# An adaLN block with latent attention and routed experts: the front part and the attention put into one block

## What is computed

```
mod = (silu(c) @ wmod).reshape(1, 6, 1, -1)
sa, ca, ga, sb, cb, gb = (mod[:, n] for n in range(6))
ga = (2 * (ga >= 0) - 1) * maximum(abs(ga), 0.25)            # gb alike
h = layernorm(x) * (1 + ca) + sa
q = rms_norm(h @ w_qa, q_a_norm_w) @ w_qb                    # 16 heads of 128 + 64
kv = h @ w_kva;  c_kv, k_rope = kv[..., :64], kv[..., 64:]
kv_up = rms_norm(c_kv, kv_a_norm_w) @ w_kvb                  # 16 heads of 128 (keys) + 128 (values)
q_rope, k_rope = apply_rope(q_rope), apply_rope(k_rope)
attn = softmax(causal(q_full @ k_full.T / sqrt(192)))
x = x + ga * ((attn @ v) @ w_o)
```

## Time and profile before

| | us |
|---|---|
| median of 3 runs | 1189.31 |
| lowest and highest | 1188.31 and 1192.61 |
| the profiled execution | 1187.94 |
| its span, first to last instruction | 1186.0 |

### The profile page before, as it was taken

One profiled execution on the slowest core, in us unless ns is written; L12 is line 12 of the kernel. 1 busy time (PEld: TensorE's weight loads), 2 busy tenths in 40 slices (PEclk: granted clock), 3 DMA queues, 4 the chain that ended last, 5 costly groups with the idle time before them and its releaser, 6 DMA issues. The chain is left out here.

```text
span 1186.0 us, 27727 instructions
## 1 busy us (share of the span) xinstructions
PE 1124.4 (95%) x11356; PEld 936.1 (79%) x11356; DVE 819.1 (69%) x1825; ACT 791.4 (67%) x1104; POOL 698.9 (59%) x579
## 2 busy tenths in 40 slices
PE   4869999999999999999999999999999878999997
PEld 4746878888888888888888888888887777989886
DVE  2758776767767777776767677776767466675776
ACT  3725777778777778778777787877877644233332
POOL 1434767678786867768777776877776762130000
PEclk8967999999999999999999999999999989999999
DMA  9250100002001000200100020011000060000000
GB/s 241 73 150 12 47 20 2 19 2 65 20 2 47 20 19 2 65 5 16 47 19 20 2 65 2 20 36 31 20 2 1 2 178 1 1 19 1 19 19 18
DMA packets 58350, 39.89 MB, mean 34 GB/s; under 512 B 8145, under 2 KB 57553, under 8 KB 58065
## 3 DMA queue, kind: packets, MB, share of 16 engines
q1 hardware_dynamic: 56832, 34.10, 10.1%
q10 hardware_dynamic: 1392, 4.03, 1.3%
HBM read 33.66 MB, written 4.46 MB: 32 GB/s over the span
## 5 line engine op out<-in xcount | busy, mean ns | idle before, releaser
L880 POOL TENSOR_TENSOR pt_lo<-pt 128x1024 f16<-128x1024 f32 x192 | 370.3, 1939 | 181.7 <-ACT pt L937 181.4
L993 DVE TENSOR_REDUCE gates<-bank 128x1 f32<-128x512 f32 x384 | 261.5, 688 | 147.7 <-PE bank L1060 144.8
L928 ACT ACTIVATE pair<-shift 128x1024 f32<-128x1024 f32 x256 | 263.4, 1029 | 12.4 <-ACT pt L941 0.7
L937 ACT ACTIVATE pt<-pair 128x1024 f32<-128x1024 f32 x192 | 196.0, 1021 | 108.6 <-PE pair L1087 107.9
L1102 PEld LDWEIGHTS bank<-values,pt 128*128 128x128 bf16 x2176 | 196.8, 98 | 80.0 <-issue 51.3
L1102 PE MATMUL bank<-values,pt 128*128 128x65 f16 x2176 | 235.2, 194 | 6.0 <-DVE lat L1019 5.1
L1104 PE MATMUL bank<-values,pt 128*128 128x64 f16 x2176 | 231.8, 192 | 0.0
L1106 PE MATMUL bank<-values,pt_lo 128*128 128x65 f16 x2176 | 230.7, 194 | 0.0
L886 POOL TENSOR_TENSOR pt_lo<-pt 128x512 f16<-128x512 f32 (+3 forms) x256 | 178.1, 721 | 45.5 <-ACT pt L941 45.4
L1104 PEld LDWEIGHTS bank<-values,pt 128*128 128x128 bf16 x2176 | 202.0, 98 | 0.0
L1106 PEld LDWEIGHTS bank<-values,pt_lo 128*128 128x128 f16 x2176 | 201.3, 97 | 0.0
(11 more groups left out here) (216 smaller groups left out, 2305.5 us busy)
## 6 DMA issues: line engine op xcount, KB each, us to landing
turn_by<-rope_cos_by_feature SPq DMA_DIRECT2D x64, 128.0 KB, 3.0
turn_by<-rope_sin_by_feature SPq DMA_DIRECT2D x64, 128.0 KB, 3.1
xs<-in_L_attn_x SPq DMA_DIRECT2D x4, 512.0 KB, 5.7
lat<-in_L_attn_w_o SPq DMA_DIRECT2D x1, 2048.0 KB, 9.6
xs_again<-in_L_attn_x SPq DMA_DIRECT2D x1, 2048.0 KB, 8.0
out<-xs_again SPq DMA_DIRECT2D x4, 512.0 KB, 2.8
lat<-in_L_attn_w_qb ACTq DMA_DIRECT2D x1, 1152.0 KB, 17.4
wq_parts<-wq_hi SPq DMA_DIRECT2D x1, 1152.0 KB, 7.2
```

The costliest lines, as they stand in the source:

```text
L880: pool.tensor_tensor(out=pt_lo[:, at].rearrange("p a n -> p (a n)"), in0=full, in1=cut(full), op=ALU.subtract).then_inc(low_ok, 1)
L928: act.activation(s_pair[u % 2][:, :, :], shift[:, item % SHIFTS:item % SHIFTS + 1, :].to_broadcast([P, 2, BW]), ACT.Copy).then_inc(seeded[ ...
L937: act.activation(pt[:, at], s_pair[u % 2][:, :, :], ACT.Exp).then_inc(exp_done, 1)
L993: dve.tensor_reduce(out=to, in_=of, axis=AXX, op=ALU.max).then_inc(work_seen["v"], 1)
```

## The change

1. `prepare` no longer has a block. It returns its engines' functions, and `attend` calls them at the head of its own streams, in one block. The barrier between the two goes; waits on single semaphores take its place.
2. SBUF: `prepare`'s buffers are put in another order and `attend`'s are laid over those that are dead early (`turn_by`, `qf`, `shift` over `xs`; the exponentials' buffers over `wq_hi` and `wq_lo`), with gaps where one would meet a live one. `q_hi`, `q_lo`, `pt`, `pt_lo`, `shift` and `spread` become several tensors. The sizes and the instructions that use them stay.
3. The query products of the first pair of heads (pairs 0 to 3) read `wq_hi` and `wq_lo` in SBUF, and not `wq` loaded back from HBM.
4. The tables of pairs 0 and 1 are issued by SP right behind w_o, once batch 1 is transposed. The store of the query weights comes behind them.
5. ACT issues w_qb and the queries' norm after `normalise(0)`, and the rest of wmod after `normalise(1)`.
6. `columns(1)` goes ahead of `low(2, 2)` on DVE. The readers of output weights 0 and 1 go ahead of `low(3, 2)`; output weights 2 and 3, with their readers, go to round -6; the opening of the score banks goes to round -3.

```diff
-        prepare(nc, sb, sem, locals())
-        attend(nc, sb, sem, locals())
+        attend(nc, sb, sem, locals(), prepare(nc, sb, sem, locals()))
...
-                act.dma_start(wqb, k["w_qb"].rearrange("p (h n) -> p h n", h=H)).then_inc(ld_qb, 16)
-                act.dma_start(qnw[:, :], k["q_norm"].rearrange("(p a) -> p a", a=1)).then_inc(ld_qn, 16)
-                act.dma_start(wm[:, :, 2 * D:], rows[:, :, 2 * D:]).then_inc(ld_rows, 16)
...
             normalise(0)
+            act.dma_start(wqb, k["w_qb"].rearrange("p (h n) -> p h n", h=H)).then_inc(ld_qb, 16)
+            act.dma_start(qnw[:, :], k["q_norm"].rearrange("(p a) -> p a", a=1)).then_inc(ld_qn, 16)
             modulate(0)
...
             normalise(1)
+            act.dma_start(wm[:, :, 2 * D:], rows[:, :, 2 * D:]).then_inc(ld_rows, 16)
             turned("v", 0)
...
+            columns(1)
             low(2, 2)
             low(3, 0)
             low(3, 1)
-                columns(1)
+            output_rows(dve, 0)
+            output_rows(dve, 1)
             low(3, 2)
...
+                before["sync"](sp)
+                weights_of = PAIRS[0][0]
                 for p, (hp, g) in enumerate(PAIRS):
+                    if p == 0:
+                        sp.wait_ge(before["xt_mm"], 2 * KD)
+                    if p == 2:
+                        before["store_query_weights"](sp)
...
+                before["scalar"](act)
                 for r in ROUNDS:
+                    if r == 0:
+                        act.wait_ge(before["wq_out"], 32)
+                        act.wait_ge(before["vl_ok"], NB)
+                        act.wait_ge(before["gate_ok"], 1)
+                        act.wait_ge(before["mod_ok"], 2)
...
+                before["vector"](dve)
                 for r in ROUNDS:
+                    if r == CHUNK_ROUND[0]:
+                        for n in (2, 3):
+                            before["output_rows"](dve, n)
+                        before["wait_side_seen"](dve, before["SIDE_AT"]["out", NP // 2 - 1])
...
                     if n >= 3:
                         wait_seen(pe, n - 3)
+                    else:
+                        before["wait_side_seen"](pe, before["SIDE_AT"]["gate", 0])
+                        pe.wait_ge(before["lo_ok"], 3 * NB - 2 + n)
...
+                    if hp == PAIRS[0][0]:
+                        w = [before[name][:, hp, part * P:part * P + P] for name in ("wq_hi", "wq_lo")]
+                    else:
+                        w = [wq[a][:, part * P:part * P + P] for a in range(2)]
...
+                before["tensor"](pe)
                 for r in ROUNDS:
+                    if r == CHUNK_ROUND[0]:
+                        for n in (2, 3):
+                            before["output_weights"](pe, n)
+                    if r == SHIFT_ROUND[0]:
+                        open_scores()
+                    if r == 2:
+                        pe.wait_ge(before["vl_ok"], NB)
+                        pe.wait_ge(before["mod_ok"], 2)
```

More of the change, by code:

```diff
@@ new lines, in output_rows, with output_weights @@
+        def output_rows(dve, n):
+            dve.wait_ge(gate_ok, 1)
+            dve.wait_ge(side_mm, SIDE_AT["out", n] + 1)
+            dve.scalar_tensor_tensor(out=w_vo[:, 2 * n:2 * n + 2, :], in0=side_of(("out", n)).rearrange("p (a n) -> p a n", a=2),
+                                     scalar=norms[:, 0:1], in1=gates[:, 0:1, :].to_broadcast([P, 2, D]), op0=ALU.mult,
+                                     op1=ALU.mult).then_inc(side_seen["v"], 1)
+        def output_weights(pe, g):
+            for j in range(4):
+                h = 4 * g + j
+                last = pe.matmul(side_of(("out", g))[(h % 2) * KVL:(h % 2) * KVL + KVL, (j // 2) * D:(j // 2) * D + D],
+                                 wv_t[:, h, :], wov[:, h, :], start=True, stop=True)
+            last.then_inc(side_mm, 1)
@@ L789, in attend @@
+        return locals()
+def attend(nc, sb, sem, k, before):
     bank, lat, ident, wq_dram, values = k["bank"], k["lat"], k["ident"], k["wq_dram"], k["values"]
@@ L834, in wait_seen, with shift_of @@
                 eng.wait_ge(work_seen[e], SEEN[e][n + 1])
+        def shift_of(item, half):
+            at = item % SHIFTS
+            return shift[at // 2][:, at % 2:at % 2 + half, :]
         def work_of(n):
@@ L866, in _ @@
             def _(pool):
+                before["gpsimd"](pool)
+                pool.wait_ge(before["side_mm"], before["SIDE_AT"]["gate", 0] + 1)
                 pool.memset(ones_r[:, :].bitcast(F32), 1.0).then_inc(consts_ok, 1)
@@ L884, in low_parts @@
                             pool.wait_ge(exp_done, OPS[u] + 1 + half)
-                            full = pt[:, at, half, live(u, half):]
-                            pool.tensor_tensor(out=pt_lo[:, at, half, live(u, half):], in0=full, in1=cut(full),
+                            full = pt[at][:, half, live(u, half):]
+                            pool.tensor_tensor(out=pt_lo[at][:, half, live(u, half):], in0=full, in1=cut(full),
                                                op=ALU.subtract).then_inc(low_ok, 1)
@@ L909, in query_high @@
                         act.wait_ge(q_sum, 2 * p + hd + 1)
[L910 removed]
+                        act.activation(q_hi[p % Q_SLOTS][:, hd, :], qf[:, hd, :], ACT.Copy).then_inc(q_hi_ok, 1)
                 def shift_rows(item):
@@ L1039, in query_products @@
                     n = WORK[("q", p, part)]
-                    if part == 0:
-                        loads = 1 + sum(a[0] != b[0] for a, b in zip(PAIRS[:p], PAIRS[1:p + 1]))
+                    if part == 0 and hp != PAIRS[0][0]:
+                        loads = sum(a[0] != b[0] for a, b in zip(PAIRS[:p], PAIRS[1:p + 1]))
                         pe.wait_ge(wq_in, 32 * loads)
```

920 lines of the change are left out of this document (458 added, 462 removed).

## The result

| | before | after |
|---|---|---|
| median, us | 1188.81 (1188.15 to 1192.61, 4 runs) | 1177.16 (1175.06 to 1179.93, 4 runs) |
| the profiled execution, us | 1187.94 | 1178.33 |
| its span, us | 1186.0 | 1176.4 |
| its mean granted clock | 0.972 | 0.985 |

The ratio is 0.9901, 95% interval 0.988 to 0.9923. The change saves 11.7 us by the medians and 9.6 us between the two profiled executions. The forecast was 6.3 us, and 1183.0 us for the time, so the sign held and nearly half of the size was missed. The forecast's own range of 1180 to 1186 us did not hold; the wide one, 1176.5 to 1187.5 us, which reaches over rivals A to C, did by 0.7 us. By the prediction's own sign it was wrong as well: the first scores shifted by 9.57 us, and more than 9 us was to mean that.

The account below looks back on a forecast made before the run. PE bounds the attention, so only its start moves: seam -5.4 us (-8.4 + 1.4 + 1.6) and front part -0.9 us give 1181.6 us profiled, plus 1.4 us for the median: 1183.0 us. Own range 1180 to 1186 us, wide 1176.5 to 1187.5 us.

Parts of the forecast that it names:

- rivals A to C: Third of them, C: gain given back by `normalise(1)`'s issue, half-clock seam and full inserts; -3.1 us, 1186.2 us; chance 0.13 with mishaps.
- the prediction's own sign: Wrong if first scores shift under 4 or over 9 us, or if that shift is not the end's.
- the opening's: Score banks' opening moved to round -3, among the maxima: four matmuls at half clock, 1.6 us lost (0 to 2.4).
- Front part, forecast -0.9 us: Start up to 36 us: later w_qb and wmod bring tokens(1) to 20.3 us; -0.9 us (+0.8 to -2).
- rival A: Front part: w_kvb clears before w_qb, tokens(1) near 15.5 us, clock may stay up; 1178 to 1181 us; chance 0.18.
- Seam, forecast -8.4 + 1.4 = -7.0 us: Front part's end to first maximum: pair 0's sum 8.4 us earlier, 1.4 us lost to readers ahead of the first maximum.
- rival E: Seam: a semaphore holds PE at part 0 until DVE finishes its output rows; +1.4 us, 1184.4 us; no separate chance.
- at most 1.4 us: Two output rows ahead of `low(3, 2)` on DVE: no cost while done before ACT's last high part, else this.
- The opening and the maxima, forecast +1.6 us: First to 17th maximum: the opening's matmuls at half clock cost 1.6 us where PE has 0.16 us to spare.
- rival B: Seam and maxima: clock stays up instead of 0.50 to 103.9 us; 3 us more gained, 1180 us; chance 0.12.
- The attention, forecast 0: From 200 to 940 us, bound by PE: the change adds or removes nothing there.
- rival D: Attention: new buffer places cost 0.04 us a unit over 320 units, 12.8 us, 1195 us; chance 0.07.

Follow-up runs that it names:

- e1: Kernel before with only the three ACT transfers put later (w_qb, queries' norm, rest of wmod): 1186.1 us, ratio 0.9967.
- e4: Changed kernel with the order of the small work undone (columns(1), output weights and readers, opening of the score banks): 1181.07 us, ratio 0.9938.
- e5: Changed kernel again, unedited, for its scatter: 1179.33 us, ratio 0.9897.
- e6: Changed kernel, with PE's first query product made to wait for the query weights' store: 1182.59 us, ratio 0.9941.
- e7: Changed kernel with 12 more matmuls, six each in rounds -5 and -4: 1178.61 us, ratio 0.9898.
- e9: Changed kernel with w_kvb and w_qb loaded in four transfers each: 1176.3 us, ratio 0.9874.
- e11: Changed kernel with the small work's order undone, plus ten extra matmuls, six in round -4 and four in round -3: 1180.64 us, ratio 0.9915.
- e12: Changed kernel with w_kvb and w_qb in four transfers each and 12 more matmuls in rounds -5 and -4: 1177.16 us, ratio 0.9878.
- e13: Changed kernel with pair 0's tables back behind the query weights' store and the last `low` products: 1184.89 us, ratio 0.9959.
- e14: Changed kernel with the four matmuls of the opening in round -3 issued twice: 1181.28 us, ratio 0.9935.
- e2: Changed kernel with the three late ACT transfers put back behind w_kvb's issue: 1178.92 us, ratio 0.9922.
- e3: Kernel before with 12 unread matmuls behind PE's last front-part instruction, keeping PE busy up to the barrier: 1190.43 us, ratio 1.0005.
- e8: Kernel before with eight more matmuls, four each in rounds -4 and -3: 1187.47 us, ratio 0.9979.
- e10: Kernel before with w_kvb and w_qb in four transfers each and nothing put later: 1187.2 us, ratio 0.9977.

## Why the prediction was right and wrong

The step that failed most is the opening's: "ahead of the stretch where PE has 0.16 us to spare. Four matmuls at half clock are 4 x 0.43 = 1.7 us: 1.6 us lost". That stretch got 2.3 us shorter in the profiled execution instead. The parts in order of time:

**Front part, forecast -0.9 us: the number came near, the steps did not.** It was -1.4 us between the two profiles, near by luck, since two errors met. The first step that failed is "w_qb is issued right behind" the last of four instructions and has its first packet 1.4 us later. It was issued at 10.07 us, 0.01 us after the *first* instruction of `normalise(0)` began, with three still to come; and its first packet came at 14.78 us, 4.7 us after the issue. (The 1.4 us was misread too: tokens(0), issued at 0.74 us, has its first packet at 1.84 us.) By then w_kvb was through, at 14.65 us. The Trainium skill, "Perfetto Trace Analysis", DVE / Act Engine Instruction, has the sequencer push an instruction to the wait queue and go on to decode the next. The trace agrees for the three that follow the first, which had no wait of their own; it doesn't for the first itself, whose wait ended at 10.06 us and held w_qb's issue until then. The second step that failed is "on the slowest of the 16 transfer engines w_qb is again straight behind w_kvb", with tokens(1) at 20.3 us. It came 0.13 us behind w_kvb's last packet, but until then it had no packet on any engine, and SP's queue had them nearly alone. In all eleven traces with the late issue (after, e1, e4 to e7, e9, e11 to e14) statistics(1) starts at 14.4 to 16.5 us; with the early issue (before, e2, e3, e8) at 21.1 to 22.5 us. This is rival A's mechanism. But A's gain of 3.2 us and more needs tokens(2) in time, and neither A nor the forecast asked when that lands: its statistics start at 24.41 us, with 4.59 us of idle time on DVE ahead. PE then waits 5.19 us, and the clock is 0.73 from 29.9 to 36 us, which A had up. At statistics(3) the nine kernels with the late issue and unsplit weights stand at 30.7 us in the mean, the four with the early one at 32.8 us: -2.1 us, where -0.9 was forecast. The earlier trace rows were the right rows; the row that was not read is the one after, tokens(2). Its transfer was issued at 12.14 instead of 19.65 us, but was under way while w_qb's packets ran, from 14.8 to 21.7 us; that these held it is likely and not shown.

**Seam, forecast -8.4 + 1.4 = -7.0 us: right in its sum.** It was -7.4 us. The steps said 66.9 us for the product and 70.45 us for the sum, without a shift in front; they started at 63.86 and 68.62 us, and the front had given 1.4 us. So the product was 1.6 us better than forecast and the sum 0.4 us. Most of the 1.6 us is the clock again, which the forecast did not ask about here: in the kernel before it was at half from 62.6 to 66.0 us, and the output weights ahead of `flip_queries(3)` took 3.32 us; in the changed kernel they took 1.95 us, from 61.59 us on. Part of it was lost again. The two readers ahead of `low(3, 2)` waited 1.27 us for the gates, so that the last `low` product started at 65.76 us, 1.0 us after its input was there (64.73 us), and PE waited 1.07 us for it, at 66.59 us. This is rival E's wait, inside the "at most 1.4 us" of the forecast. The readers ahead of the first maximum took 1.39 us for 1.4 forecast. e13 and e6 price what was one term: by the means the early tables are worth 6.9 us and the reading in place 5.1 us. They don't add, since either one alone late holds the sum. That the seam came out to 0.4 us is thus in part luck.

**The opening and the maxima, forecast +1.6 us: wrong in sign, and the largest miss.** The duration was right: four matmuls at half clock, 1.7 us forecast, 1.91 us measured, and e14's second set cost 1.7 us more. Missed was the other side: that work on PE in this stretch brings the clock back. Two pairs that differ in such work alone show the return: 15.5 us after the first maximum in e4 and 4.1 us in e11, 17.3 us in the kernel before and 6.4 us in e8. The forecast held the clock at 0.50 until the scores, by the earlier trace rows, and counted matmuls there as costs alone. First to 17th maximum took:

| kernels | 17th less first maximum, us | clock |
|---|---|---|
| before, e1, e3, e4, e10 | 27.2, 26.6, 27.1, 26.7, 27.2 | back 15 to 17 us after the first maximum |
| after, e2, e6, e9 | 24.9, 24.9, 24.9, 24.9 | back within 8 us, no second fall |
| e11, e12 | 25.5, 25.2 | back within 5 us, no second fall |
| e5, e13, e8, e14 | 26.8, 26.7, 27.7, 28.5 | back early, second fall |
| e7 | 23.8 | up throughout |

So -2.3 us with one fall, and about -0.4 with two, in place of +1.6. The price of the clock rests on these profiled executions, one for each kernel, above all on the two of the changed kernel itself (24.9 and 26.8 us). The times of all runs bear it out less well: e7 and e11 gained 0.5 and 0.7 us with 1 us of scatter, e8 2.5 us, and e14 lost 2.8 us. The forecast reckoned with full clock and with half clock for the whole stretch (rival B and itself), but not with a clock that falls and comes back 10 us sooner. The argument against B, "PE in the stretch of the maxima is held by DVE, and at full clock it would be idle for more than half of it", turned out too strong: from 85 to 90 us PE is busy for 4.09 of 5 us at full clock with DVE at 4.66. The Trainium skill, "TensorE: Matmul & The Clock Gate", HAM oscillation, blames idle gaps for the throttle; closing one gap (e3) put the fall off by 6.8 us here and gained no time, filling the maxima (e7) kept the clock up throughout, and only the latter agrees with the page in full.

**The attention, forecast 0: right in its rows.** No cost of new places (rival D): the matmuls of values take 192 ns before and after, the subtraction on POOL 1939 and 1940 ns.
```profile
L912 POOL TENSOR_TENSOR pt_lo<-pt 128x1024 f16<-128x1024 f32 x192 | 370.4, 1940 | 182.1 <-ACT pt L969 181.8
...
L1158 PE MATMUL bank<-values,pt 128*128 128x64 f16 x2176 | 231.8, 192 | 0.0
```
The 1.3 us that the profile lost there came at the attention's end, where the clock fell from 920.1 to 923.6 us:
```profile
920.00:925.00 5.00, 5.00 (x41) 3.80 (x39) 2.14 (x6) 1.51 (x2) 1.38 (x2) 0.66 0.02 3
```
The shift against before was 11.1 us at the 17th maximum and 11.2 us at 279 and 490 us, and 9.8 us behind that fall. Nine traces have it (after, e1, e4, e5, e7, e8, e9, e11, e14) and take 820.6 to 821.6 us from the 17th to the last maximum; the seven without it (before, e2, e3, e6, e10, e12, e13) take 819.5 to 820.2 us. What brings it on stays open. The first scores (9.57 us) and the end (9.6 us) shifted alike only because of it and of the maxima: in between it was 11.2 us.

**From the profile to the median.** The forecast added 1.4 us for the distance of the median from the profiled execution; this time the median lay 1.2 us below. Of the 5.8 us between forecast and median this is 2.6; 3.9 are the opening's stretch, 0.5 the front, 0.4 the seam, and the late fall takes 1.5 back (sum 5.9). With runs that scatter by 2 us, the 2.6 us are not a mechanism to be found. And the split holds for this one profile: with e5's, of the same program, the opening's stretch would be 2.0 us off and not 3.9.

## What to carry to other kernels

When a late transfer is brought forward, look up the next one on the same queue before booking the gain: here a step of 5 us on tokens(1) left 2 us, since tokens(2) moved by less. A stretch in which PE runs at half clock though another engine sets the pace has two prices for work that must be done somewhere: its own duration, and the clock that it brings back sooner; moving needed work there gained 3.4 us (e4 undone, its shorter path included), while adding work for the clock alone gained between 0 and 2.5 us, and once lost 2.8 us. Where several things are ready late at one point, each is worth nearly the whole wait (6.9 and 5.1 us of 7.4), so they have to be moved together and can't be priced by their sum.

## What the runs showed of the hardware

- A transfer that ACT issued behind another still under way had its first packet late: w_qb, issued at 10.07 us, at 14.78 us, while SP's queue moved 1075 packets from 12 to 15 us. In the nine traces with the late issue and unsplit weights it is 3.8 to 5.2 us from issue to first packet, and w_kvb's last packet had ended 0.1 to 1.4 us before. Issued early (2.90 us, the kernel before), w_qb had its first packet at 11.48 us, ahead of w_kvb's last, which ended at 14.24 us. Whether the late one waits for w_kvb or for something else stays open.
- A transfer's issue that follows a waiting instruction on ACT's stream is held by that instruction's wait (10.07 after 10.06 us), not by the instructions of the same step behind it, which ran until 12.1 us.
- One program had one fall of the clock in one profiled execution (77.1 to 83.9 us) and two in another (74.6 to 81.4 and 84.8 to 91.7 us), and first to 17th maximum took 24.9 and 26.8 us. Over all runs of it the time at half clock was 37.7 us in the mean, where the kernel before had 63.6 us. How much of the 11.7 us is the clock's is read from the maxima (2 to 2.5 us with one fall) and not from these 26 us: e3 took 5 us off the time at half clock (58.2 instead of 63.6 us) and gained nothing.
